# Weight pack in two transfers around the first context half, products of ones in the first waits, composition in its own bank, query products in four tiles

## The reference, cut to what matters

```python
# layer 0, attention: v = context @ Wq, q = x_normed @ Wq (8 channels)
corr = real(ifft(fft(q) * conj(fft(k)))).mean(batch, channel)
W_topk, I_topk = top_k(corr, 11); W_topk = softmax(W_topk)
R = sum(w * roll(v, -shift) for w, shift in zip(W_topk, I_topk)); y = repeat(R, heads) @ Wout + bout
# layer 0, feed-forward: two composed matrices (rank 64, 32 primitives)
W1 = einsum('k,kir,kro->io', softmax(top_k(fc1_logits)), A1, B1)   # 128 x 512
W2 = einsum('k,kir,kro->io', softmax(top_k(fc2_logits)), A2, B2)   # 512 x 128
h  = gelu(x1 @ W1) @ W2
# layer 1, attention: keys and values from the context
K = ctx @ Wk + bk ; V = ctx @ Wv + bv ; out = softmax(Q K^T / sqrt(D)) V @ Wo + bo
```

## Time and profile before

| | us |
|---|---|
| median of 3 runs | 335.76 (335.49 to 336.69) |
| the profiled execution, its own time | 337.2 |
| its span | 335.0 |
| TensorE busy | 315.0 (94% of the span) |
| VectorE busy | 262.3 (78%) |
| ScalarE busy | 201.6 (60%) |
| loads into the core up to the end of the preparation | 16.55 MB read from HBM |

### The profile page before, as it was taken

The page is one execution under the profiler, slowest core; times in us unless marked ns, Lnnn a source line. Parts: engine busy times, 40 slices in busy tenths (PEclk is TensorE's granted clock), DMA queues, the critical chain, the costliest instruction groups (busy, mean ns, idle before and its releaser), DMA issues.

```text
span 335.0 us, 4438 instructions
## 1 busy us (share of the span) xinstructions
PE 315.0 (94%) x1498; PEld 224.1 (67%) x1506; DVE 262.3 (78%) x543; ACT 201.6 (60%) x325; POOL 45.8 (14%) x55
## 2 busy tenths in 40 slices
PE   7999899899999899969879999999999999998995
PEld 7655698556556667656657777777767777766763
DVE  2542674769578997979987989989987996999693
ACT  3514206464687856688878758758367546635733
POOL 0030012121111701164171121000001000000000
PEclk9899999999999999999979999999999999999999
DMA  7999960000000000180440651001001000000001
GB/s 261 427 422 317 297 257 1 0 3 0 0 0 2 1 2 0 63 190 1 132 120 1 179 104 33 0 2 32 0 0 34 0 0 31 3 0 31 2 0 63
DMA packets 13173, 25.21 MB, mean 75 GB/s; under 512 B 608, under 2 KB 9056, under 8 KB 11872
## 3 DMA queue, kind: packets, MB, share of 16 engines
q1 hardware_dynamic: 11712, 20.75, 17.5%
q0 software_dynamic: 1440, 4.19, 6.8%
HBM read 16.55 MB, written 1.05 MB: 53 GB/s over the span
## 4 chain that ended last, share of the span: by engine, by line
PE 80%; DVE 8%; ACT 6%; issue 3%; DMA 2%; POOL 0%; SPq 0%; DVEq 0%; ACTq 0%; POOLq 0%
PE ps L1389 76%; DMA ctxT<-in_ctxT 2%; PE ps L1495 1%; PE ps L1612 1%; ACT ring L560 1%; ACT L610 1%; ACT L575 1%; ACT L560 1%; DVE hm_even L1070 1%; PE ps L1516 1%; ACT hid L612 1%; ACT hB L552 1%; DVE ctxT L1281 1%; DVE kv L1278 1%; DVE ctxT L1280 1%
## 5 line engine op out<-in xcount | busy, mean ns | idle before, releaser
L1389 PE MATMUL ps<-hm_even,ew_hi 128*128 128x512 f32 (+1 forms) x152 | 49.6, 420 | 1.9 <-ACT xi L538 1.2
L1389 PE MATMUL ps<-hm_odd,ew_hi 128*128 128x512 f32 (+1 forms) x148 | 47.6, 422 | 0.0
L1389 PEld LDWEIGHTS ps<-hm_even,ew_hi 128*128 128x128 f32 (+1 forms) x152 | 26.3, 188 | 8.4 <-issue 2.4
L1389 PEld LDWEIGHTS ps<-hm_odd,ew_hi 128*128 128x128 f32 (+1 forms) x148 | 25.7, 189 | 5.5 <-issue 0.5
L612 ACT ACTIVATE hid<-ps,pB 128x512 f32<-128x512 f32 x32 | 21.8, 687 | 11.6 <-PE ps L1389 10.9
L477 POOL TENSOR_TENSOR zz<-zz,mhalf 128x4 f32<-128x4 f32 x12 | 14.8, 1237 | 91.2 <-DVE zz L943 91.2
L1389 PE MATMUL ps<-hm_even,ew_lo 128*128 128x512 f32 (+1 forms) x72 | 25.2, 392 | 0.0
L1389 PE MATMUL ps<-x_hi,w1x_hi 128*128 128x512 f32 x40 | 19.1, 478 | 5.8 <-ACT hid L612 3.7
L1389 PE MATMUL ps<-hm_odd,ew_lo 128*128 128x512 f32 (+1 forms) x64 | 22.3, 394 | 0.0
L1051 DVE SCALAR_TENSOR_TENSOR ring<-ring,pB,hid 128x1024 f32<-128x1024 bf16 x16 | 20.5, 1281 | 0.6
L1389 PE MATMUL ps<-zz,pB 128*128 128x512 f32 (+3 forms) x52 | 19.4, 502 | 0.5 <-DVE zz L1324 0.5
(11 more groups left out here) (325 smaller groups left out, 769.0 us busy)
## 6 DMA issues: line engine op xcount, KB each, us to landing
ring<-in_fc1b SPq DMA_DIRECT2D x4, 1024.0 KB, 17.3
ring<-in_fc2a SPq DMA_DIRECT2D x4, 1024.0 KB, 12.4
hm_odd<-hm_odd SPq DMA_DIRECT2D x4, 512.0 KB, 3.1
packC<-in_packC SPq DMA_DIRECT2D x1, 1152.0 KB, 9.1
pB<-in_packB SPq DMA_DIRECT2D x1, 1077.0 KB, 9.9
ctxT<-in_ctxT SPq DMA_DIRECT2D x2, 512.0 KB, 6.4
a<-in_fc1a SPq DMA_DIRECT2D x1, 1024.0 KB, 8.9
xtok<-in_xtok SPq DMA_DIRECT2D x1, 1024.0 KB, 12.8
```

The costliest lines, as they stand in the source:

```text
L1389: return pe.matmul(out, lhsT, rhs, start=start, stop=stop)
```

## The change

- The columns of the weight pack are reordered, so that what the value and key products need comes first (661 of 1242 columns, or 330 KB by the row's 621), and the pack is loaded in two transfers: the first as before at the head, the second (`in_spec`: logits, transform matrices, Wout) behind the first context half.
- VectorE builds `wqm`/`wqc` and the small bias values first; the maxima of the logits wait for `in_spec` ahead of the first `k8` copy; the primitive weights come after the second group's copies; the four scalings of `a1` come after all six groups.
- ScalarE copies `wvo` and `wqk` first, then takes the exponentials, then the values, then `cw`.
- TensorE has two products of ones ahead of its wait for `wqc` and three ahead of the value products; `cl`·`wout` and `sl`·`wout` move behind the value products.
- The W1 composition accumulates in bank 1 and waits for the copy of `cw`, no more for the last key's copy, which is waited for ahead of `compose_w2(0)`.
- The query products are four to a slot at k = 3 to 6, where they were two to a slot at k = 1 to 8.
- `spectral_out` stands before the ninth product of `compose_w2(0)`, where it stood before the thirteenth.

```diff
-PACK_A = [("wv", 128, D), ("wq8", 128, DH), ("u", 128, 1), ("bq8", 128, DH), ("log1", 128, PRIM),
-          ("log2", 128, PRIM),
-          ("wout", 128, D), ("cl", 128, NF), ("sl", 128, NF), ("cf", NF, S), ("sf", NF, S),
-          ("a1", NF, 1), ("a2", NF, 1), ("bout", 128, 1), ("ident", 128, 128),
+PACK_A = [("wv", 128, D), ("wq8", 128, DH), ("u", 128, 1), ("bq8", 128, DH),
           ("bk", 128, 1), ("bq", 128, 1), ("wkT", 128, D), ("wqT", 128, D), ("wo", 128, D), ("bv", 128, 1),
-          ("bo", 128, 1)]
+          ("bo", 128, 1), ("ident", 128, 128),
+          ("log1", 128, PRIM), ("log2", 128, PRIM), ("a1", NF, 1), ("a2", NF, 1), ("bout", 128, 1),
+          ("cl", 128, NF), ("sl", 128, NF), ("sf", NF, S), ("cf", NF, S), ("wout", 128, D)]
@@ block.sync
-            for dst, src, name in ((pA[:, :], d_packA, "in_A"),
+            kv_cols = colA["log1"][1]
+            for dst, src, name in ((pA[:, 0:kv_cols], d_packA[:, 0:kv_cols], "in_A"),
                                    (ctxT[:, 0:T // 2], d_ctxT[:, 0:T // 2], "in_ctx_0"),
+                                   (pA[:, kv_cols:nA], d_packA[:, kv_cols:nA], "in_spec"),
                                    (ctxT[:, T // 2:T], d_ctxT[:, T // 2:T], "in_ctx_1"),
@@ block.scalar
+            act.wait_ge(sem("wvo_ps"), 1)
+            act.activation(A("wv"), bank[6][:, 0:D], ACT.Copy).then_inc(sem("wvo"), 1)
+            act.wait_ge(sem("bvo_ps"), 2)
+            act.activation(wqk, bank[5][:, 0:D], ACT.Copy).then_inc(sem("wvo"), 1)
             act.wait_ge(sem("lgn"), 2)
             for i, n in enumerate(("log1", "log2")):
                 act.activation(lg_e[:, i, :], A(n), ACT.Exp, bias=lg_n[:, i:i + 1],
                                accum_out=lg_n[:, 2 + i:3 + i]).then_inc(sem("lge"), 1)
+            for g in range(VG):
...
             act.wait_ge(sem("cw_ps"), 1)
             act.activation(cw[:, :, :], bank[1][0:NF, 0:2 * D].rearrange("p (a d) -> p a d", a=2),
                            ACT.Copy).then_inc(sem("cw"), 1)
-            act.wait_ge(sem("wvo_ps"), 1)
-            act.activation(A("wv"), bank[6][:, 0:D], ACT.Copy).then_inc(sem("wvo"), 1)
-            act.wait_ge(sem("bvo_ps"), 2)
-            act.activation(wqk, bank[5][:, 0:D], ACT.Copy).then_inc(sem("wvo"), 1)
-            for g in range(VG):
...
@@ block.vector
             dve.wait_ge(sem("in_A"), 16)
-            for i, n in enumerate(("log1", "log2")):
-                dve.tensor_reduce(lg_n[:, i:i + 1], A(n), AX.X, ALU.max, negate=True)\
-                    .then_inc(sem("lgn"), 1)
...
             dve.wait_ge(sem("bvo_ps"), 2)
             dve.tensor_copy(bgk[:, :], bank[4][:, 0:1]).then_inc(sem("bvo"), 1)
+
+            dve.wait_ge(sem("in_spec"), 16)
+            for i, n in enumerate(("log1", "log2")):
+                dve.tensor_reduce(lg_n[:, i:i + 1], A(n), AX.X, ALU.max, negate=True)\
+                    .then_inc(sem("lgn"), 1)
...
                 dve.tensor_copy(ccol[:, b0:b0 + nb], vk_bank(g)[:, 0:nb, D + DH]).then_inc(sem("k8"), 1)
-                if g >= VG - 4:
-                    scale_a1(g - (VG - 4))
+                if g == 1:
+                    primitive_weights()
+            for i in range(4):
+                scale_a1(i)
@@ block.tensor
             pe.wait_ge(sem("in_A"), 16)
-            mm(bank[1][0:NF, 0:D], A("cl"), A("wout"))
-            mm(bank[1][0:NF, D:2 * D], A("sl"), A("wout")).then_inc(sem("cw_ps"), 1)
             mm(bank[0][:, 256:264], ones[:, :], A("wq8"))
             mm(bank[6][:, 0:D], A("wv"), A("wo")).then_inc(sem("wvo_ps"), 1)
             mm(bank[7][:, 0:1], A("wo"), A("bv"))
             mm(bank[7][:, 1:2], A("wkT"), A("bq")).then_inc(sem("bvo_ps"), 1)
+            for _ in range(2):
+                mm(bank[3][:, 0:128], ones[:, :], ones[:, :])
             pe.wait_ge(sem("wqc"), 1)
             mm(bank[4][:, 0:1], wqc, A("bk"))
             mm(bank[5][:, 0:D], A("wkT"), wqc).then_inc(sem("bvo_ps"), 1)
+            for _ in range(3):
+                mm(bank[3][:, 0:128], ones[:, :], ones[:, :])
...
                 last.then_inc(sem("v_ps"), 1)
+            pe.wait_ge(sem("in_spec"), 16)
+            mm(bank[1][0:NF, 0:D], A("cl"), A("wout"))
+            mm(bank[1][0:NF, D:2 * D], A("sl"), A("wout")).then_inc(sem("cw_ps"), 1)
...
-            pe.wait_ge(sem("k"), NCH)
+            pe.wait_ge(sem("cw"), 1)
             for k in range(KC):
...
-                last = mm(bank[6][:, :], a1[:, k, :], b1_piece(i)[:, k % KP, :], start=k == 0, stop=k == KC - 1)
+                last = mm(bank[1][:, :], a1[:, k, :], b1_piece(i)[:, k % KP, :], start=k == 0, stop=k == KC - 1)
...
-                if 1 <= k <= B // 2:
+                if 3 <= k <= 6:
                     pe.wait_ge(sem("in_x"), 16)
-                    for b in (2 * k - 2, 2 * k - 1):
+                    for b in range(4 * k - 12, 4 * k - 8):
...
             pe.wait_ge(sem("v"), VG)
-            compose_w2(0, {12: spectral_out})
+            pe.wait_ge(sem("k"), NCH)
+            compose_w2(0, {8: spectral_out})
```

More of the change, by code:

```diff
@@ L433, in _ @@
         def _(pool):
-            pool.memset(mhalf[:, :], -0.5).then_inc(sem("mhalf"), 1)
+            pool.memset(mhalf[:, :], -0.5).then_inc(sem("ones"), 1)
             pool.memset(ones[:, :], 1.0).then_inc(sem("ones"), 1)
             pool.memset(minus_1[:, :], -1.0).then_inc(sem("minus_1"), 1)
-            pool.wait_ge(sem("mhalf"), 1)
+            pool.wait_ge(sem("ones"), 1)
             pool.wait_ge(sem("veps"), 1)
@@ L503, in _ @@
                                accum_out=lg_n[:, 2 + i:3 + i]).then_inc(sem("lge"), 1)
-            act.wait_ge(sem("cw_ps"), 1)
-            act.activation(cw[:, :, :], bank[1][0:NF, 0:2 * D].rearrange("p (a d) -> p a d", a=2),
-                           ACT.Copy).then_inc(sem("cw"), 1)
-            act.wait_ge(sem("wvo_ps"), 1)
-            act.activation(A("wv"), bank[6][:, 0:D], ACT.Copy).then_inc(sem("wvo"), 1)
-            act.wait_ge(sem("bvo_ps"), 2)
-            act.activation(wqk, bank[5][:, 0:D], ACT.Copy).then_inc(sem("wvo"), 1)
             for g in range(VG):
@@ L517, in _ @@
                     .then_inc(sem("v"), 1)
+            act.wait_ge(sem("cw_ps"), 1)
+            act.activation(cw[:, :, :], bank[1][0:NF, 0:2 * D].rearrange("p (a d) -> p a d", a=2),
+                           ACT.Copy).then_inc(sem("cw"), 1)
             act.wait_ge(sem("bvo"), 3)
@@ L529, in _ @@
             act.wait_ge(sem("w1_ps"), 1)
-            act.activation(w1[:, :], bank[6][:, :], ACT.Copy).then_inc(sem("w1"), 1)
+            act.activation(w1[:, :], bank[1][:, :], ACT.Copy).then_inc(sem("w1"), 1)
             act.wait_ge(sem("y_ps"), 1)
@@ L819, in _ @@
             dve.tensor_scalar(cen, ident, -1.0 / D, None, ALU.add).then_inc(sem("wqc"), 1)
[L820 to L826, removed]
             dve.wait_ge(sem("bvo_ps"), 1)
@@ L832, in _, with primitive_weights @@
             dve.tensor_copy(bgk[:, :], bank[4][:, 0:1]).then_inc(sem("bvo"), 1)
+            dve.wait_ge(sem("in_spec"), 16)
+            for i, n in enumerate(("log1", "log2")):
+                dve.tensor_reduce(lg_n[:, i:i + 1], A(n), AX.X, ALU.max, negate=True)\
+                    .then_inc(sem("lgn"), 1)
+            def primitive_weights():
+                dve.wait_ge(sem("lge"), 2)
+                link(dve.reciprocal(lg_n[:, 4:6], lg_n[:, 2:4]))
+                for i in range(2):
+                    for half in range(2):
+                        p = slice(64 * half, 64 * half + 64)
+                        dve.tensor_scalar(wcol[p, i, :], lg_e[p, i, half:PRIM:2], lg_n[p, 4 + i:5 + i], None,
+                                          ALU.mult).then_inc(sem("wcol"), 1)
             def scale_a1(i):
@@ L886, in _ @@
                 .then_inc(sem("spec"), 1)
-            dve.wait_ge(sem("ones"), 1)
+            dve.wait_ge(sem("ones"), 2)
             dve.wait_ge(sem("spec"), 6)
@@ L1389, in mm @@
                 return pe.matmul(out, lhsT, rhs, start=start, stop=stop)
-            pe.wait_ge(sem("ones"), 1)
+            pe.wait_ge(sem("ones"), 2)
             for _ in range(8):
@@ L1452, in spectral_out @@
                 pe.wait_ge(sem("abf"), 2)
-                pe.wait_ge(sem("cw"), 1)
                 mm(bank[4][:, 0:128], cw[:, 0, :], ab_f[:, 2, :], stop=False)
```

## The result

The changed kernel takes 1.0064 of the time of before (95% interval 1.0042 to 1.0086): slower by 2.1 us where 0.5 us less was forecast. Its four executions took 338.02, 344.97, 337.72 and 344.78 us, median 341.4; before, 335.62. The two above 344 us are left out of the ratio; their mean granted clock is 0.975, that of the others 0.994 and 0.999. The execution profiled took 338.02 us (span 335.9), against 337.2 (span 335.0) of the profiled one of before.

The account below looks back on a forecast made before the run. TensorE was taken to bound nearly all of the first 70 us. Correlation 1.5 us earlier, less 0.95 for spectral_out's place, gave 0.5 to 0.6: profiled 337.2 to 336.7, median 335.76 to 335.3; range 333.9 to 337.2 (own case 334.9 to 336.0).

Parts of the forecast that it names:

- Value products at 7.2: TensorE's value products start at about 7.2 us (before 7.30); at the high clock all 16 need 4.1 us.
- composition at 16.1: The W1 composition starts at 16.1 us, not 18.01, since bank 1 needs no key copy.
- the chain from correlation to `spectral_out`: VectorE's chain from the correlation to spectral_out takes 5.51 us, putting spectral_out at 39.4.
- the standstill of 2.3: TensorE arrives ahead of spectral_out at 37.1 us and waits 2.3 us, against 1.37 before.
- `ln_tok` near 42.7: With eight products behind spectral_out, ln_tok starts at 42.7 us against 43.2 before.
- the size of the gain, 1.5 us: The correlation starts at 33.9 us, 1.5 us earlier; with spectral_out at 12 the whole gain would be 1.5.
- b1's second piece was put at 20.9: The composition's fifth product (k = 4) waits 0.5 us for b1's second piece, landing at 20.9, 0.3 either way.
- the place at 8: Moving spectral_out before the ninth product of compose_w2(0) leaves eight products behind it, not four, and costs 0.95 us.
- from there the order is the old one and the chain is TensorE's: Past ln_tok the order is unchanged and TensorE's products set the time, leaving the sum's gain at 0.5 to 0.6 us.
- A: Later waits absorb the 0.95 us of spectral_out's forward place, so the gain is 1.5 us: 334.3; chance 0.17.
- B: The clock still falls among the value products, costing 1.7 us there; sum +0.7: 336.4, up to 337.5; chance 0.20.
- C: The pack's added transfer is not hidden, delaying all behind it up to 2.2 us; sum +1.7: 337.4; chance 0.10.

Follow-up runs that it names:

- early_dft: spec12 with the forward transform at k = 8, not 10, and the correlation at k = 12, not 14; ratio 0.9963, median 335.20 us.
- fill_gap: The changed kernel, spectral_out still at 8, with nine products of ones filling the standstill ahead of its wait; ratio 1.0055, median 337.76 us.
- spec12: The changed kernel with spectral_out back before the thirteenth product of compose_w2(0); ratio 0.9994, median 335.46 us.
- early_order: The changed kernel with spectral_out behind all 16 products, b1's second piece loaded ahead of xT, query slots at k = 5 to 8; 0.9987, 336.00 us.
- queries_first: As queries_mixed, but all sixteen query products ahead of the composition, transform at k = 5, correlation at k = 9; ratio 0.9984, median 336.36 us.
- delay4: spec12 with four products of ones between center_w1 and ln_tok; ratio 1.005, median 338.27 us.
- delay8: spec12 with eight products of ones between center_w1 and ln_tok; ratio 1.0074, median 338.76 us.
- no_ones: spec12 without the five products of ones; ratio 1.0013, median 336.65 us.
- one_transfer: spec12 with the weight pack in one transfer at the head, columns in the new order; ratio 0.9998, median 336.33 us.
- two_slots: spec12 with the query products two to a slot at k = 1 to 8, as before; ratio 1.0005, median 336.88 us.
- before16: The kernel before with only spectral_out moved behind all 16 products of compose_w2(0); ratio 0.9994, median 335.50 us.
- after_again: The changed kernel run once more, with no further edit; ratio 1.0063 to the kernel before, median 338.42 us.
- queries_mixed: The changed kernel, xtok and xT loaded before b1, eight queries ahead of the composition, transform at k = 6, spectral_out ahead of compose_w2(0); 0.9988, 335.79 us.

## Why the prediction was wrong

**Steps that held.** Value products at 7.2 (6.76) at the high clock; composition at 16.1 (16.32); four queries at 0.224 each, so a slot of 1.75 (1.74); the wait for b1 as what comes late next; the chain from correlation to `spectral_out` 5.51 (40.44 - 34.89 = 5.55); the standstill of 2.3 (2.31); `ln_tok` near 42.7, or within 0.3 to 0.5 of it in the two traces of after without a fall ahead of it (42.97, 43.16). A second context half that lands at 9.2 gave TensorE a wait of 0.93 at 9.26 that I had not foreseen; the copies cover it.

**The first step that failed: the size of the gain, 1.5 us.** Two terms of it. The start was 18.01 and the end 43.2, read from one execution with a fall among the values; without a fall, as in two thirds of before's executions, they are 17.72 and 42.92. This takes 0.3. And b1's second piece was put at 20.9 with 0.3 either way, from the earlier trace rows; it landed later: products that waited for it started at 21.18 to 22.55 in nine traces of after and its variants. SyncE's issue of it starts between 4.64 and 5.82 us in them (4.72 in after), but a later issue does not go with a later landing (4.77 and 22.40 in early_dft, 5.82 and 21.77 in fill_gap), so why it is late stays open. Before never waited there, so that its trace holds no bound for that lateness but the one landing. This takes 0.3 to 1.6, in spec12, at 21.50, 0.6. What was left measured 0.2 us on the time (spec12) and 42.92 - 42.39 = 0.5 in the trace.

**The second: the place at 8, sized 0.95 on the whole time.** In the trace the step itself was right, 0.9 us from the correlation to `ln_tok`. On the time it costs 1.0063 - 0.9994 of before, 2.3 us (338.42 - 335.46 = 3.0 by the medians), and 1.0073, 2.4 us, where it is the only edit. The two terms make up the miss: -0.55 + (1.5 - 0.2) + (2.3 - 0.95) = 2.1. The step that failed is the sentence "from there the order is the old one and the chain is TensorE's". The order is, and a delay ahead of `ln_tok` does come through at its full size; but the time of the products is not fixed. 16 of 19 executions of after have a fall of the clock somewhere, 3 of 12 of spec12, and at 1.1 to 1.6 us a fall this is some 0.7 to 0.9 us. So the sum had the falls at nothing, without a reason: the fall at 171.3 stood in the trace of before that I used, and I looked at the clock only in the first 12 us. The other 0.4 to 0.7 us of the term are in no trace.

**Rivals.** A (the place is free and all of 1.5 us arrives): wrong on both halves. B (the clock falls among the values): in no trace of after or its variants, though TensorE stood idle for 0.93 us there in after. A related thing does occur: in the traces of early_order, queries_first, delay4, delay8 and no_ones the high level comes only at about 10 us, not at 4 to 6. C (the added transfer isn't hidden): one_transfer took as long as spec12, so it is hidden. The Trainium skill, "DMA: Bandwidth & Descriptors", section "Anatomy of one DMA", has a fixed 2 us for each transfer, measured on those issued by GpSimd, and would have put them on it; for a transfer queued behind others no run here agrees.

The case that happened had no rival: executions differ in their falls and in what they lose ahead of 43 us, and the place at 8 goes with the worse ones. One late fall of 1.2 us on top of the forecast gives 336.5, and b1 0.8 us later 337.3, just outside the range; 335.76 x 1.0064 = 337.9 is what the ratio gives.

**What stays open.** Whether and why an order that is late by 1 us makes a fall more likely; what the typical executions of after lose beyond the 0.9 us and the fall, perhaps the late first rise told below; and whether the runs of several falls need the wait for b1, the four-product slots, or both, since two_slots changed only one of them.

## What to carry to other kernels

Profile the kernel before several times, or at least read the granted clock over the whole span, before an edit's gain is read from one trace: a trace with two falls is the exception here, and the one among the values overstated what could be won by 0.3 us. An edit that ends a wait in one queue ends at the next thing that nobody waited for yet, and the old trace holds no bound for that: here b1's landing. Where executions differ by falls of the clock, take the time from a stage to the end in several traces: here it is the same within 0.1 us for one order of the work, but for a fall, so that it tells what an edit did from what the execution had anyway. A delayed kernel and its partner are to be run on the same chip. And for a wait like that ahead of `spectral_out`, moving its producers forward won (early_dft), while moving its consumer forward lost (the place at 8).

## What the runs showed of the hardware

**One standstill, two outcomes.** TensorE stood still for 2.00 to 2.09 us near 170 us in all twenty traces, with the same instructions around it. The clock stayed up in twelve and fell 0.1 to 1.5 us behind its end in eight (before, before16, after_again, fill_gap, delay4, delay8, two_slots, queries_mixed). Neither the length (2.00 to 2.08 in the twelve, 2.04 to 2.09 in the eight) nor the time tells them apart: it ended at 169.5 to 177.6 us in the twelve, at 169.0 to 173.3 in the eight. The Trainium skill, "TensorE: Matmul & The Clock Gate", section "HAM oscillation — how this bites in real kernels", says that waits between bursts bring the low clock back. The traces agree that they can, here behind waits of about 2 us, and show that the same wait need not.

**The mean clock doesn't count the low level before the first rise.** In no_ones the stretch from 7 to 8 us is given as 1.00:

```profile
7.00:8.00 1.00, 1.00 (x6) 1.00 (x6) 0.34 (x3) 0.49 (x2) 0.00 (x0) 1.00 1.12 389
7.16 3.63 PE L1395 MATMUL ps<-pA,ctxT 128*128 128x137 f32 x18
```

But nine products take 3.63 us, 0.40 each, where after's six take 1.57, 0.26 each, and the mean clock of this execution is given as 1.000. The duration of a known product tells the level there; the clock's column doesn't.

This late first rise costs, too. The traces of no_ones, delay8, delay4 and early_order, with the high level from about 10 us on, reach the correlation at 35.61 to 36.01 us, that of spec12, with it from about 5.3 us on, at 34.56: 1.0 to 1.4 us sooner. This fits two groups that the mean clock doesn't tell apart. The executions of early_order without a fall took 334.01 to 334.99 and 336.28 to 336.66 us, and the traced one is of the second group (336.48). Those of one_transfer took 334.91 to 335.34 and 336.69 to 336.95, five each, and 13 of before's 86 took 336.51 to 336.70, where the rest stayed under 336.2; a late one was traced of neither. After's executions with one fall spread as widely, from 337.11 (high level from 4.4 us on) to 339.12; whether those above 338.1 rose late was not traced.
